# A feed-forward stage with a seven-product block algorithm for W1 and PSUM sums for W2

## The reference

```python
h = jax.nn.gelu(flat_x @ W1 + b1)      # 1024 x 512 @ 512 x 2048, tanh form
y = h @ W2                             # 1024 x 2048 @ 2048 x 512
y = jnp.nan_to_num(y, nan=0.0, posinf=0.0, neginf=0.0)
x = x + y + b2
```

## Time and profile before

| | |
|---|---|
| median of 3 runs | 2133.66 us (2133.07 to 2134.09) |
| profiled execution, span | 2132.0 us; its own time is not recorded apart, the median is 1.7 above the span |
| PE busy | 2052.8 us (96%) |
| DVE busy | 1501.1 us (70%) |
| ACT busy | 1017.1 us (48%) |
| POOL busy | 548.4 us (26%) |
| DMA | 76.87 MB, mean 36 GB/s |
| mean granted clock of PE | 0.988 of 2.4 GHz |

### The profile page before, as it was taken

The page is one execution under the profiler, slowest core; times in us unless marked ns, Lnnn a source line. Parts: engine busy times, 40 slices in busy tenths (PEclk is TensorE's granted clock), DMA queues, the critical chain, the costliest instruction groups (busy, mean ns, idle before and its releaser), DMA issues.

```text
span 2132.0 us, 33393 instructions
## 1 busy us (share of the span) xinstructions
PE 2052.8 (96%) x11352; PEld 1763.7 (83%) x11352; DVE 1501.1 (70%) x2365; ACT 1017.1 (48%) x2232; POOL 548.4 (26%) x428
## 2 busy tenths in 40 slices
...
DMA packets 44161, 76.87 MB, mean 36 GB/s; under 512 B 7379, under 2 KB 13651, under 8 KB 43603
## 3 DMA queue, kind: packets, MB, share of 16 engines
...
...
## 4 chain that ended last, share of the span: by engine, by line
PE 87%; DVE 7%; issue 3%; ACT 2%; DMA 0%; SPq 0%; DVEq 0%; ACTq 0%
PE bank L1085 22%; PE bank L1087 22%; PE bank L1086 22%; PE bank L1145 9%; PE bank L1190 6%; PE bank L1258 1%; PE bank L1341 1%; PE bank L1259 1%; PE bank L1340 1%; PE bank L1315 1%; DVE negmax L870 1%; DVE V_lo L864 1%; DVE pT_lo L908 1%; DVE q_lo L902 1%; DVE stats L768 0%
## 5 line engine op out<-in xcount | busy, mean ns | idle before, releaser
L880 DVE SCALAR_TENSOR_TENSOR xacc<-bank,rinv,xacc 128x512 f32<-128x512 f32 x512 | 375.9, 745 | 71.5 <-PE bank L1087 71.3
L486 ACT ACTIVATE pT_hi<-bank 128x512 fp32r<-128x512 f32 x320 | 190.7, 597 | 202.4 <-PE bank L1190 202.1
L870 DVE TENSOR_REDUCE negmax<-bank 128x1 f32<-128x640 f32 x256 | 210.2, 821 | 37.2 <-PE bank L1145 30.0
L540 ACT ACTIVATE prob<-bank,negmax 128x640 f32<-128x640 f32 x256 | 202.6, 791 | 66.7 <-DVE negmax L870 66.7
L908 DVE TENSOR_TENSOR pT_lo<-bank,pT_hi 128x512 fp32r<-128x512 f32 x320 | 217.6, 680 | 2.4 <-ACT pT_hi L486 2.4
L1190 PE MATMUL bank<-ident,prob 128*128 128x128 f32 x1280 | 191.3, 272 | 0.0
L1190 PEld LDWEIGHTS bank<-ident,prob 128*128 128x128 f32 x1280 | 159.2, 140 | 18.7
L383 POOL TENSOR_TENSOR wo_lo<-wo_raw,wo_hi 128x512 fp32r<-128x512 f32 x32 | 41.4, 1293 | 428.4 <-ACT wo_hi L486 428.4
L1085 PE MATMUL bank<-xwv_hi,cT_hi 128*128 128x256 f32 x512 | 144.2, 282 | 3.1 <-DVE xV_lo L928 3.1
L626 ACT ACTIVATE xprob<-xscore,negmax 128x128 f32<-128x128 f32 x256 | 99.5, 391 | 95.9 <-DVE negmax L961 95.9
L1086 PE MATMUL bank<-xwv_lo,cT_hi 128*128 128x256 f32 x512 | 143.8, 281 | 0.0
...
## 6 DMA issues: line engine op xcount, KB each, us to landing
...
```

The costliest lines, as they stand in the source:

```text
L486: return s.activation(dst, src, ACT.Copy)
L540: s.activation(prob[:, slot, i, :].rearrange("p (a t) -> p a t", a=2), S_bank[i % 2], ACT.Exp, bias=negmax[:, slot, i:i + 1], scale=1.0, a ...
L870: v.tensor_reduce(negmax[:, slot, i:i + 1], S_bank[i % 2], mybir.AxisListType.XY, ALU.max, negate=True).then_inc(a["max"], 1)
L880: v.scalar_tensor_tensor(xacc[:, 4 * half + i, :], M, rinv[:, k, i:i + 1], xacc[:, 4 * half + i, :], ALU.mult, ALU.add).then_inc(sems["y"], 1)
```

## The change

Hidden features and input features are cut into two halves, and so are the tokens. A group g (0 to 7) is one pair of hidden tiles, 2g and 2g+1, for all 1024 tokens: four blocks C11, C12, C21, C22 of 128 x 512 (the second index is the token half; C11 and C21 are tiles 2g and 2g+1 of the first half). Instead of 8 block products (48 PE instructions) PE makes 7 (P1 to P7, 6 instructions each, 42), of sums and differences of the blocks of W1 and of x:

- x: xf keeps the transposed x in float32 (a second ACT copy per tile, x_first and x_second). DVE makes the four differences T (128x1024 each, in place in xf), ACT and DVE split them (t_hi, t_lo). xB holds blocks and one difference, xS the other three.
- W1: early weights are tile 2g (early, we_raw; split by early_hi and early_lo), for P1 and P2. Late weights are both tiles again (late_weights, 512 KB), from which POOL makes four sums (late_sums, 128x256 each); ACT and POOL split five blocks at once (late_hi, late_lo, 128x1280), for P3 to P7.
- The products meet on DVE and ACT: p1_copy brings P1 into part; c11 = P2 + P1; u2 = P6 + P1; u3 = P7 + u2; u4 = P5 + u2; c22 = P5 + u3; c12 = P3 + u4; c21 = P4 + u3. Each reads one PSUM bank and one SBUF tile.

Hidden tiles of the first token half are multiplied with W2 at once (y0, 12 PE instructions, summed in four banks over all 16 tiles; FIRST and LAST are two token tiles each); those of the second half are kept (hid1) and multiplied at the end, token tile by token tile, over all 16 hidden tiles, with a second load of W2 (again, split into w2all by ACT and by DVE or, every third, POOL). yacc, its memset and its 128 additions go; finish(b) checks, sums and selects from the bank, on DVE alone. b2 is added to xacc by POOL one token tile per group. b1's 16 loads now stand in one go ahead of early(2). All buffers of the stage have fixed addresses; semaphores of the first attention are used again with an offset (f_after: P1 waits on the name a_q, wolo means c12, rot means c22, y means u3, Khi means c21, S and max mean the sums).

```diff
+NG = NF // 2
+HALF_S = [0, 1, 2, 3, 4, 6, 8, 10]
+LATE_S = [5, 7, 9, 11, 12, 13, 14, 15]
+Y_ORDER = [0, 2, 4, 6, 8, 1, 10, 3, 12, 5, 14, 7, 9, 11, 13, 15]
...
+            early(0)
+            early(1)
+            second(0)
+            second(1)
+            for n in range(NF):
+                sp.dma_start(b1_sb[:, n:n + 1], b1[n]).then_inc(s_b1, 16)
+            early(2)
+            sp.wait_ge(c["wo"], LAST1)
+            late_weights(0)
             sp.dma_start(b2_sb[:, :], b2.partition_broadcast(P)).then_inc(s_b, 16)
...
+            early(3)
+            second(2)
+            second(3)
+            early(4)
+            second(4)
+            for g in range(NG):
+                if g + 1 < NG:
+                    late_weights(g + 1)
+                if g + 5 < NG:
+                    early(g + 5)
+                if g < 2:
+                    for n in range(4 * g, 4 * g + 4):
+                        again(n)
+                for s_ in (5 + 2 * g, 6 + 2 * g) if g < 3 else (8 + g,):
+                    if s_ < NF:
+                        second(s_)
+            for n in range(8, NF):
...
+            def late_sums(n):
+                pool.wait_ge(s_wlraw, 16 * (n + 1))
+                if n:
+                    pool.wait_ge(f["wlhi"], f0["wlhi"] + n)
+                    pool.wait_ge(f["wllo"], f0["wllo"] + n)
+                g.tensor_tensor(wl_f[:, 4], wl_f[:, 2], wl_f[:, 3], ALU.add).then_inc(f["S0"], 1)
+                g.tensor_tensor(wl_f[:, 6], wl_f[:, 0], wl_f[:, 2], ALU.subtract)
+                pool.wait_ge(f["S0"], f0["S0"] + 2 * n + 1)
+                g.tensor_tensor(wl_f[:, 5], wl_f[:, 4], wl_f[:, 0], ALU.subtract).then_inc(f["S0"], 1)
+                pool.wait_ge(f["S0"], f0["S0"] + 2 * n + 2)
+                g.tensor_tensor(wl_f[:, 7], wl_f[:, 1], wl_f[:, 5], ALU.subtract).then_inc(f["S"], 1)
+            def late_lo(n):
+                pool.wait_ge(f["wlhi"], f0["wlhi"] + n + 1)
+                g.tensor_tensor(wl_lo[:, n % 2], wl_f[:, 3:8], wl_hi[:, n % 2], ALU.subtract).then_inc(f["wllo"], 1)
+            early_lo(0)
+            early_lo(1)
+            second_lo(0)
+            early_lo(2)
+            second_lo(1)
...
             pool.wait_ge(c["wo"], LAST1)
...
+            late_sums(0)
+            late_lo(0)
+            early_lo(3)
+            second_lo(2)
+            second_lo(3)
+            early_lo(4)
             pool.wait_ge(s_b, 16)
...
+            for n in range(NG):
+                if n + 1 < NG:
+                    late_sums(n + 1)
+                    late_lo(n + 1)
+                if n + 4 < NG:
+                    second_lo(HALF_S[n + 4])
+                if n + 5 < NG:
+                    early_lo(n + 5)
+                second_lo(LATE_S[n])
+                if n == 0:
+                    pool.wait_ge(L[3, "xn"], B)
+                g.tensor_tensor(xacc[:, n, :], xacc[:, n, :], b2_sb[:, :], ALU.add).then_inc(s_xb, 1)
+            for n in range(2, NF, 3):
+                pool.wait_ge(f["ahi"], f0["ahi"] + n + 1)
+                g.tensor_tensor(w2all_lo[:, n], w2_again[:, n % 8], w2all_hi[:, n], ALU.subtract)\
+                 .then_inc(f["alo2"], 1)
...
+            def late_hi(g):
+                act.wait_ge(f["S"], f0["S"] + g + 1)
+                if g >= 2:
+                    act.wait_ge(f["P4"], f0["P4"] + g - 1)
+                copy(wl_hi[:, g % 2], wl_f[:, 3:8]).then_inc(f["wlhi"], 1)
+            def x_first(b):
+                act.wait_ge(L[3, "tr"], b + 1)
+                copy(xB_hi[:, 0:2, :, cols], src.rearrange("p (k c n) -> p k c n", k=2, c=2)).then_inc(L[3, "hi"], 1)
+                copy(xf[:, 0, :, cols], src.rearrange("p (c n) -> p c n", c=C)).then_inc(f["xf"], 1)
...
+            def t_hi(n, dst, src):
+                act.wait_ge(f["T"], f0["T"] + n)
+                copy(dst, src).then_inc(f["Thi"], 1)
...
             ln_sqrt(3, 1)
...
+            for b in range(4):
+                x_first(b)
             ln_sqrt(3, 2)
...
+            p1_copy(0)
+            p1_copy(1)
+            act.wait_ge(s_b1, 16 * NF)
+            hidden_early(0)
+            early_hi(3)
+            x_second(4)
+            x_second(5)
+            hidden_early(1)
+            p1_copy(2)
+            x_second(6)
+            x_second(7)
+            late_hi(0)
+            t_hi(1, xB_hi[:, 3], xf[:, 0, 0:2])
+            second_hi(2)
+            t_hi(2, xS_hi[:, 0], xf[:, 1, 2:4])
+            t_hi(3, xS_hi[:, 1], xf[:, 1, 0:2])
+            p1_copy(3)
+            t_hi(4, xS_hi[:, 2], xf[:, 0, 2:4])
+            hidden_early(2)
+            early_hi(4)
+            second_hi(3)
+            hidden_early(3)
+            for g in range(NG):
+                if g + 1 < NG:
+                    late_hi(g + 1)
+                if g + 4 < NG:
+                    second_hi(HALF_S[g + 4])
+                    p1_copy(g + 4)
+                hidden_second(g, "c22", "g22", 2 * g + 1, late[:, 2])
+                if g + 4 < NG:
+                    hidden_early(g + 4)
+                if g + 5 < NG:
+                    early_hi(g + 5)
+                hidden_second(g, "c12", "g12", 2 * g, late[:, 1])
+                second_hi(LATE_S[g])
+                hidden_late(g)
...
+            c11(0)
+            x_second_lo(4)
+            x_second_lo(5)
+            h_lo(0)
+            c11(1)
+            x_second_lo(6)
+            x_second_lo(7)
+            dve.wait_ge(f["xf"], f0["xf"] + B)
+            v.tensor_tensor(xf[:, 0, 0:2], xf[:, 1, 0:2], xf[:, 0, 0:2], ALU.subtract).then_inc(f["T"], 1)
+            dve.wait_ge(f["T"], f0["T"] + 1)
+            link(v.tensor_tensor(xf[:, 1, 0:2], xf[:, 1, 2:4], xf[:, 1, 0:2], ALU.subtract))
+            v.tensor_tensor(xf[:, 1, 2:4], xf[:, 1, 2:4], xf[:, 0, 0:2], ALU.subtract).then_inc(f["T"], 2)
+            dve.wait_ge(f["T"], f0["T"] + 3)
+            v.tensor_tensor(xf[:, 0, 2:4], xf[:, 0, 2:4], xf[:, 1, 2:4], ALU.subtract).then_inc(f["T"], 1)
+            t_lo(1, xB_lo[:, 3], xf[:, 0, 0:2], xB_hi[:, 3])
+            h_lo(1)
+            c11(2)
+            t_lo(2, xS_lo[:, 0], xf[:, 1, 2:4], xS_hi[:, 0])
+            t_lo(3, xS_lo[:, 1], xf[:, 1, 0:2], xS_hi[:, 1])
+            t_lo(4, xS_lo[:, 2], xf[:, 0, 2:4], xS_hi[:, 2])
+            h_lo(2)
+            c11(3)
+            h_lo(3)
...
+            for g in range(NG - 1):
+                u2(g)
+                u4(g)
+                u3(g)
+                c22(g)
+                if g + 4 < NG:
+                    c11(g + 4)
+                    h_lo(HALF_S[g + 4])
+                c12(g)
+                c21(g)
+                h_lo(LATE_S[g])
+            u2(NG - 1)
+            u3(NG - 1)
+            u4(NG - 1)
+            c22(NG - 1)
+            c21(NG - 1)
+            c12(NG - 1)
+            h_lo(LATE_S[NG - 1])
...
+            dve.wait_ge(f["P4"], f0["P4"] + NG)
+            for q in range(4):
+                for n in range(4 * q, 4 * q + 4):
+                    if n % 3 != 2:
+                        again_lo(n)
+                    if n == 4 * q:
+                        hid1_lo_split(0, q)
+            dve.wait_ge(f["y0"], f0["y0"] + NF)
+            for q in range(4):
+                hid1_lo_split(1, q)
+            for b in range(4):
+                finish(b, Y_bank[b])
+            for q in range(4):
+                hid1_lo_split(2, q)
+            dve.wait_ge(f["y1"], f0["y1"] + 1)
+            finish(4, Y1_bank[0])
+            for q in range(4):
+                hid1_lo_split(3, q)
+            for b in range(5, B):
+                dve.wait_ge(f["y1"], f0["y1"] + b - 3)
+                finish(b, Y1_bank[b - 4])
...
+            def p6(g):
+                pe.wait_ge(f["wllo"], f0["wllo"] + g + 1)
+                if g == 0:
+                    pe.wait_ge(f["Tlo"], f0["Tlo"] + 4)
...
+                product(p6_bank(g), late_w(g, 2), xs(0)).then_inc(f["P6"], 1)
...
+            p1(0)
+            p2(0)
+            p1(1)
+            transpose_second(4)
+            transpose_second(5)
+            p2(1)
+            p1(2)
+            transpose_second(6)
+            transpose_second(7)
+            y0(0, EVERY)
+            p2(2)
+            p1(3)
+            y0(1, EVERY)
+            p2(3)
+            y0(2, EVERY)
             pe.wait_ge(L[3, "lo"], B)
...
+            for g in range(4):
+                fill = 3 if g == 0 else LATE_S[g - 1]
+                p6(g)
+                y0(fill, FIRST)
+                p5(g)
+                p1(g + 4)
+                p7(g)
+                p2(g + 4)
+                p3(g)
+                y0(fill, LAST)
+                p4(g)
+                y0(HALF_S[g + 4], EVERY)
+            p6(4)
+            for g in range(4, NG - 1):
+                p5(g)
+                y0(LATE_S[g - 1], FIRST)
+                p7(g)
+                p6(g + 1)
+                p3(g)
+                y0(LATE_S[g - 1], LAST)
+                p4(g)
+            p7(NG - 1)
```

(11 more changed lines are left out.)

489 lines of the change are left out of this document (321 added, 168 removed), and 3 rows, old and new, of the table f_after.

## The result

The changed kernel takes **2146.39 us** (median of 4 runs, 2142.97 to 2149.82) against 2133.36 (4 runs, 2131.31 to 2134.09): ratio 1.0066, 95% interval 1.0052 to 1.0081, or 13.0 us slower. The forecast was 2149.7 in a range of 2134 to 2161. The profiled execution is the fastest of the four (2142.97 us, span 2141.2), 3.4 us under their median; the one of the kernel before (2133.66 us, span 2132.0) is not the fastest of its own.

A forecast was written before the change was run, and what follows sets the result against it. It took PE as busy throughout the feed-forward stretch, then POOL's queue and DVE's SBUF-only splits as setting the new waits. Savings and waits summed to +16.0 on 2133.7, giving 2149.7 us, range 2134 to 2161.

The forecast's parts named there:

- W1's products: Feed-forward stage on PE: W1 goes from 384 products to 336 at 0.2333 us each; -11.2 us.
- tail: After the last product: yacc additions go, seven of eight finishes lie beside later products; 5.3 us instead of 15.7, -10.4.
- pause before the last half unit: PE's wait for DVE of about 1.0 us at 2113.44 goes; -1.0 us.
- entry: old pause, new waits: Stage entry: old 1.9 us pause replaced; late_lo(0), early_lo(3) and DVE's SBUF-only list delay p6(0); -1.9 and +14.6 us.
- groups 0 to 3: p3 waits 0.3 us each for the bank c22 reads; late hidden tile has PE cover; +1.2 us.
- groups 4 to 6, with the clock: POOL's queue makes p6(g+1) wait for late_lo(g+1), rounds 15.8 us, +14.6; one clock fall of two, +2.5.
- end: After P4(6): y0(15) waits for h_lo(15), +5.8; second W2 split on DVE and POOL, +2.4; +8.2 us in all.
- Rival (b): Groups 4 to 6: only the hidden tile's chain binds, 14.6 becomes 5, no clock fall; 2137.6 us; chance 0.22.
- rival (c): Clock falls at every long wait: p6(5), p6(6), p6(7), y0(15), the entry; 2.5 us each; 2159.7 us; chance 0.18.
- Rival (a): POOL's splits stay ahead of PE throughout the stage; waits shrink from 41.1 to 17 us; 2126 us; chance 0.10.
- Part 1: W1's products in the feed-forward stage: 336 instead of 384, W2 stays at 384; -11.2 us.
- part 2: Sums stay in PSUM, so yacc additions go: tail -10.4 us, DVE pause before the last half unit -1.0.

The follow-up runs named there:

- e8: Changed kernel plus six unread products behind p3 in each of groups 0 to 3; one run, 2148.44 us against 2142.97 for the changed kernel's profiled run.
- e2: Changed kernel with POOL's additions of b2 for tiles 3 to 7 moved behind its part of the second W2 split; 2142.74 us.
- e3: e2 with second_hi of the late units, from group 3 on, ahead of c22's gelu on ACT; 2139.52 us.
- e1: Changed kernel with early_lo(3) ahead of late_lo(0) in POOL's queue at the entry; 2148.73 us.
- e10: e7 with late_hi(0) on ACT right behind the third layernorm's square root and late_lo(0) on POOL ahead of the b2 additions; 2128.20 us.
- e12: e10 plus nine unread products before p1(0), with two b2 additions ahead of early_lo(3) and six spread over the first three groups; 2122.92 us.
- e5: e1 with DVE doing h_lo and c11 between the four differences and hidden_early(2) earlier on ACT; 2145.86 us.
- e6: Changed kernel with unread products filling PE's waits before p1(3), y0(1), p6(5) to p6(7), y0(12), y0(13) and y0(15); 2145.42 us.
- e4: Changed kernel with e5's entry, reordered b2 additions and second_lo(3) on POOL, second_hi and hidden_late(7) earlier on ACT; 2129.38 us.
- e7: e4 with PE walking the second W2 pass for token tiles 0 and 1 together; 2126.96 us.

## Why the prediction was right

Its sum, term by term, against the changed kernel's profiled execution. In the forecast the sum stood against a span of 2132.0, and the span is 9.2 us longer. The changed kernel's execution also reached the stage 3.0 us earlier (the third layernorm's first statistics start at 1910.8 instead of 1913.8, in code that is the same in both), so that 9.2 + 3.0 = 12.2 us are to be explained.

| term | forecast | measured | from |
|---|---|---|---|
| W1's products | -11.2 | -11.2 | 720 products; price confirmed by e8 for groups 0 to 3 |
| tail | -10.4 | -10.9 | 15.7 to 4.8 |
| pause before the last half unit | -1.0 | -1.0 | |
| start of p1(0) | -0.6 | -0.9 | statistics to p1(0) 15.25, was 16.16 |
| entry: old pause, new waits | -1.9, +14.6 | -1.9, +13.1 | 36.98 - 19.6 - 1.9 - 2.4 |
| groups 0 to 3 | +1.2 | +0.8 | P4(3) ends 59.6 us after p6(0) begins; 58.8 of products |
| groups 4 to 6, with the clock | +14.6, +2.5 | +16.6 | 50.2, less 33.6 of products |
| end | +8.2 | +7.6 | 63.6 from P4(6), less 56.0 |
| sum | +16.0 | +12.2 | |

- **Products and tail: right.** e8 shows that a product counts in full in groups 0 to 3. In groups 4 to 6 it could not, as POOL set the rounds (e2, e3); the table counts it there too, and the waits with it.
- **Entry: right in size, half right in cause.** The prediction put the wait on early_lo(3) "queued behind" late_lo(0). p1(3) did wait for it (6.2 us), but e1 shows that DVE's list was as late. The exclusion from the earlier trace rows held for 1280 columns: I took the 2.98 and not the 1.29, and the row shows 3.80 for a 1.22 us instruction. By the Trainium skill ("SBUF — State Buffer", section "SBUF: two separate sides") one holder keeps the shared port for its whole instruction; the trace agrees, in both directions (early_lo(3) took 2.24 behind DVE's difference). e10 and e12 show it at three more places.
- **Groups 4 to 6: right in mechanism.** POOL's chain ended at P4 + 9.7 in the profile (2065.50 less 2055.8, where P4(5) ended, 0.95 before c21's gelu), 10.1 in the forecast. The rounds were 16.9 and not 15.8: 0.4 less by the chain, and 1.5 more by the fall of the clock inside the round, as e2's round of 14.00 prices it. Rival (b), that POOL's queue does not bind, is refuted by e2 and e3, where POOL does the same work in another order and the rounds shorten.
- **The clock: the step that was mis-sized in its parts.** I took one fall on the path, rival (c) all of them. Five came after p1(0), the number that (c) had, but not quite at its places (behind y0(13) and not behind p6(5)), and only two were on the path (p6(6) and p6(7), 1.4 each by 7 x 0.195), which is 2.8 for the 2.5 taken. That the two figures are so close is partly luck: with the fall behind p6(5) that e1 and e5 had, it is 1.5 more. The Trainium skill ("TensorE: Matmul & The Clock Gate", section "HAM oscillation — how this bites in real kernels") warns of lulls that each send the array back to half clock. Five of the waits did so here; three of these falls cost nothing, because the engine that released PE next was not waiting for PE (e6). Whether a given wait brings a fall was not steady: the same 2.30 us before p6(5) gave 1.00 in one kernel and 0.50 in two others.
- **End: +5.8 for y0(15) was nearly right** (h_lo(15) ended 14.7 us after P4(6), at the upper end of what I gave). The 2.4 for the second W2 split did not appear: y0(15) came so late that the splits were ahead. (The forecast's own figures, 14.7 + 15.5, give 30.2 and not 30.6, so that the term was 0.4 too high by them.) It did appear as soon as the rounds became shorter (e2, e4), and e7 took it away.
- **Rival (a), POOL ahead of PE and the change faster**, had 2126 for it. It was not so in this kernel, but it was in reach: e4 and e7 change no product, no split and no difference, only orders, and are faster than the kernel before (by 0.14% and 0.23%).

What stays open: why the clock falls behind one wait and not behind an equal one, and what moves the start of p1(0) by up to 3.5 us from run to run. The table explains the fastest of four executions; what the median one has beyond it (3.4 us) no profile shows. More falls of the clock, as in e1 and e5, would have that size, which is argued and not shown. Part 1 without part 2 was not tried, so that the seven-product form and the sums in PSUM are priced by the sum above and not by runs of their own.
